# Gate logits of a four-expert layer computed with the activations as the loaded operand of TensorE

## What is computed

```python
gate_logits = jnp.einsum('bte,en->btn', x, Wg) + bg      # x: 1250 x 768, Wg: 768 x 4
top = jnp.argmax(gate_logits, axis=-1)                   # the expert of each node
h = gelu(einsum(x, W1) + b1);  y = einsum(h, W2) + b2    # per expert
out = the y of the expert that was chosen
```

## Time and profile before

| | us |
|---|---|
| median of 3 runs | 1021.78 (1020.6 to 1023.49) |
| the profiled execution | 1026.36 |
| span of its profile | 1024.5 |
| PE busy in the span | 989.0 (97%) |
| DVE busy | 598.0 (58%) |
| ACT busy | 312.9 (31%) |
| stage of the gates, first wait of PE after the heads to the first use of the gates on DVE | 451.0 to 478.07 |
| from there to the first transpose of the expert layer | 478.07 to 491.2 |

### The profile page before, as it was taken

The page is one execution under the profiler, slowest core; times in us unless marked ns, Lnnn a source line. Parts: engine busy times, 40 slices in busy tenths (PEclk is TensorE's granted clock), DMA queues, the critical chain, the costliest instruction groups (busy, mean ns, idle before and its releaser), DMA issues.

```text
span 1024.5 us, 15870 instructions
## 1 busy us (share of the span) xinstructions
PE 989.0 (97%) x5707; PEld 799.3 (78%) x5707; DVE 598.0 (58%) x1264; ACT 312.9 (31%) x888; POOL 67.5 (7%) x134
## 2 busy tenths in 40 slices
PE   7999999999999999999899999999999999999997
PEld 5777678999999999986566665667997557888884
DVE  7887799999999999995223237541111112333231
ACT  2444353665565566433111121221111110110100
POOL 2100000000000000132222211000000000000000
PEclk9999999999999999999999999999999999999999
DMA  6000010111111111016772539123001005001101
GB/s 160 2 1 1 1 55 4 48 39 38 38 48 46 52 37 37 13 59 248 219 265 86 185 124 287 46 75 118 1 1 46 1 1 171 26 30 31 31 12 51
DMA packets 40017, 69.99 MB, mean 68 GB/s; under 512 B 21074, under 2 KB 24926, under 8 KB 39448
## 3 DMA queue, kind: packets, MB, share of 16 engines
q1 hardware_dynamic: 37321, 58.85, 18.3%
q0 software_dynamic: 2080, 10.23, 3.0%
q10 hardware_dynamic: 559, 0.16, 0.1%
HBM read 50.10 MB, written 19.12 MB: 68 GB/s over the span
## 4 chain that ended last, share of the span: by engine, by line
PE 89%; DVE 4%; issue 2%; ACT 1%; DMA 1%; POOL 0%; ACTq 0%; DVEq 0%; POOLq 0%; SPq 0%
PE O L961 19%; PE pw L1127 15%; PE pc L831 8%; PE pa L1156 7%; PE O L958 6%; PE pw L1189 6%; PE ph L1052 5%; PE py L1073 5%; PE pa L1201 3%; PE pf L796 3%; PE pw L1215 2%; PE pf L831 2%; PE O L898 1%; PE pct L808 1%; PE pt L1117 1%
## 5 line engine op out<-in xcount | busy, mean ns | idle before, releaser
L961 PE MATMUL O<-X,masks 125*125 125x264 f32 x1200 | 277.5, 331 | 0.0
L958 PE MATMUL O<-X,CSR 125*125 125x132 f32 x1080 | 244.1, 226 | 0.0
L961 PEld LDWEIGHTS O<-X,masks 125*125 125x125 f32 x1200 | 220.1, 186 | 0.1
L1779 DVE SCALAR_TENSOR_TENSOR masks<-a2b,NA,CSR 125x375 fp32r<-125x375 f32 (+1 forms) x360 | 212.1, 649 | 6.3 <-PE O L961 4.8
L958 PEld LDWEIGHTS O<-X,CSR 125*125 125x125 f32 x1080 | 203.3, 188 | 0.0
L2040 DVE SCALAR_TENSOR_TENSOR UL<-pw,dinv,UH 125x768 fp32r<-125x768 f32 x20 | 20.4, 1018 | 109.6 <-ACT UH L1513 109.6
L1127 PE MATMUL pw<-W 128*125 128x384 f32 x240 | 80.8, 494 | 1.0 <-ACT W L1506 1.0
L831 PE MATMUL pc<-ohs_a,ohd 125*125 125x512 f16 x375 | 78.6, 349 | 1.6 <-DVE ohs_a L1589 1.6
L1127 PE MATMUL pw<-region,xr_or_h 128*125 128x384 f32 x240 | 77.6, 486 | 0.0
L1127 PEld LDWEIGHTS pw<-region,xr_or_h 128*125 128x125 f32 x240 | 45.0, 188 | 32.1
L1127 PEld LDWEIGHTS pw<-W 128*125 128x125 f32 x240 | 45.0, 191 | 31.8 <-issue 2.8
(11 more groups left out here) (252 smaller groups left out, 1441.8 us busy)
## 6 DMA issues: line engine op xcount, KB each, us to landing
a2b<-a_rows SPq DMA_DIRECT2D x12, 610.4 KB
W<-in_L_ffn_W SPq DMA_DIRECT2D x4, 1152.0 KB
WM<-in_L_ffn_W SPq DMA_DIRECT2D x4, 1152.0 KB
xr_or_h<-in_x SPq DMA_DIRECT2D x10, 336.0 KB
XH<-in_x SPq DMA_DIRECT2D x12, 280.0 KB
z_rows<-region SPq DMA_DIRECT2D x10, 336.0 KB
region<-y_rows SPq DMA_DIRECT2D x10, 336.0 KB
x_rows<-xr_or_h SPq DMA_DIRECT2D x10, 336.0 KB
```

Of the source, the lines that this page charges most:

```text
L958: nc.tensor.matmul(O[0:P, bank, d - d0, 2 * DP:4 * DP], CSR[:, s, d * P:(d + 1) * P], X[:, buf, s, 4:6, :].rearrange("p k d -> p (k d)"), ...
L961: ins = nc.tensor.matmul(O[0:P, bank, d - d0, 0:4 * DP], kept, X[:, buf, s, 0:4, :].rearrange("p k d -> p (k d)"), start=s == 0, stop=s == ...
L1779: nc.vector.scalar_tensor_tensor(masks[:, s, 0:(d1 - d0) * P], a2b[:, buf, d0 * P:d1 * P], NA1[:, s, bass.ds(h, 1)], CSR[:, s, d0 * P:d1 * ...
```

## The change

`gates(t)` exchanges the operands: the turned tile, 128 x 125, is loaded, and `WG` with its four columns moves. The result is nodes by experts, 125 x 4, and is written at once to its four columns of `pg`. `copy_gates`, `turn_gates`, the buffer `gT` and the semaphores `s_gc3` and `s_gt3` go. DVE (line 1694 of the new file) and SP (before it loads the experts' second biases, line 615) wait for `s_g3` of the last tile in place of `s_gt3`.

```diff
-        gT = in_side(448, N, NEXP)
...
-        s_gc3, s_gt3 = sem("gates_copied"), sem("gates_turned")
...
-                sp.wait_ge(s_gt3, NT)
+                sp.wait_ge(s_g3, NT)
...
                 def gates(t):
 
                     pe.wait_ge(s_ztc3, 2 * t + 2)
-                    if t >= 2:
-                        pe.wait_ge(s_gc3, t - 1)
                     for k in range(KF):
-                        ins = nc.tensor.matmul(pgt[0:NEXP, t % 2, 0:P], WG[:, k, :], ZT[:, t % 2, k, :],
+                        ins = nc.tensor.matmul(pg[0:P, NEXP * t:NEXP * (t + 1)], ZT[:, t % 2, k, :], WG[:, k, :],
                                                start=(k == 0), stop=(k == KF - 1))
                     ins.then_inc(s_g3, 1)
-
-                def turn_gates(t):
-
-                    pe.wait_ge(s_gc3, t + 1)
-                    nc.tensor.transpose(pg[0:P, NEXP * t:NEXP * (t + 1)], gT[:, t * P:(t + 1) * P],
-                                        ident[0:NEXP, 0:NEXP]).then_inc(s_gt3, 1)
...
                         gates(t)
-                        if t:
-                            turn_gates(t - 1)
-                    turn_gates(NT - 1)
...
-                def copy_gates(t):
-                    act.wait_ge(s_g3, t + 1)
-                    nc.scalar.copy(gT[:, t * P:(t + 1) * P], pgt[0:NEXP, t % 2, 0:P]).then_inc(s_gc3, 1)
...
                         copy_zt(t)
-                        copy_gates(t - 1)
-                    copy_gates(NT - 1)
...
-                    dve.wait_ge(s_gt3, NT)
+                    dve.wait_ge(s_g3, NT)
```

## The result

| | us | |
|---|---|---|
| median before, in the same comparison | 1022.63 | 4 runs, 1020.6 to 1023.49 |
| median after | 1034.47 | 4 runs, 1033.03 to 1036.15 |
| ratio after / before | 1.011 | 95% interval 1.0093 to 1.0128 |
| profiled execution after, its span | 1033.65, 1031.9 | before 1026.36, 1024.5 |
| mean granted clock of the runs | 0.978 to 0.980 | profiled execution before 0.994 |

The account below looks back on a forecast made before the run. PE was taken to bound the gates stage. At low clock: tiles +12.4, last gates +1.1, tail -0.65, sorting +0.7, perhaps half a microsecond back; 1021.8 + 13.3 gives about 1035 us, range 1018 to 1037.

Parts of the forecast that it names:

- (e): Gates stage: streaming falls from 81% to 32% of a tile; judged by streaming, the clock stays low; 1035 us, chance 0.50.
- Step (d): Gate instructions: bound by loads, twelve take 1.32 us at clock 1.0 (1.38 now), 2.52 at 0.5 (2.48 now).
- rival 3: Gates stage: clock stays low but loads keep 0.11 us; 2.72 us a tile, +1.7, 1023.5 us; chance 0.05.
- The term of a tile: Gates stage at low clock: transposes 1.40 plus gates 2.52, 3.92 us, 1.55 more than now; eight cycles, +12.4.
- The sorting: Fourteen line 923 matmuls start at low clock: 1.5 us extra, less 0.8 us of cover, +0.7.
- the second fall: Clock drop at about 487.5 before the change; if it doesn't happen, half a microsecond at the expert layer comes back.
- (b): Gates stage: the small transpose of line 905 leaves PE, 0.19 us a tile, eight times on the path.
- (c): End of the gates stage: the tail between last gate instruction and DVE goes; 0.65 us saved, about 0.08 left.
- Rival 4: Gates stage: path not shortened because normalised tiles, stores or biases are late; 1021 to 1022 us; chance 0.04.
- rival 1: Gates stage: loads count as work, clock returns and holds; 2.11 us a tile, -2.8, 1019.0 us; chance 0.34.

Follow-up runs that it names:

- e6: Kernel before, with 20 matmuls of 4 moving columns (loads of 125) in TensorE's wait ahead of the gates stage: 1023.24 us, ratio 1.0008 to the kernel before.
- e1: Kernel before, with nine filler matmuls of 512 columns in TensorE's wait ahead of the gates stage: 1020.79 us, ratio 0.9975 to the kernel before.
- e4: Changed kernel with gates of three of the six feature blocks only, six loads fewer a tile: 1018.32 us, single run, whole time not compared.
- e2: Changed kernel with nine fillers of 512 columns ahead of the gates stage: 1028.94 us, ratio 1.0059 to the kernel before.
- e7: Kernel before with nine fillers ahead of the stage and exchanged operands in every second tile: 1020.39 us, ratio 0.9981 to the kernel before.
- e3: As e2, plus two fillers of 512 columns after each tile's gates: 1036.54 us, ratio 1.0104 to the kernel before.
- e5: As e2, plus four fillers a tile, two after the transposes and two after the gates: 1029.37 us, ratio 1.0066 to the kernel before.

## Why the prediction was right

**The cause, (e), was right.** The clock didn't come back in the stage, as forecast for a chip that goes by streaming. The prediction could not tell from the trace of before whether loads count and gave this case a chance of a half, so choosing it was in part a bet; e6 against e1 settles it. The rows that it leaned on, the fall after 484.1 to 487.3 and the rise only after unbroken streaming, pointed the right way. Two of its readings are weaker than they sound. It counts a transpose's 0.107 us as streaming, but each transpose also loads 128 columns (PEld), so its shares of streaming are upper ones. And the earlier trace rows show that transposes held a clock that was up (609.2 to 613.4), not that they raise one: beside loads they didn't raise it in the 40.6 us here.

**Step (d) was right.** Loads end 0.21 us apart at 0.5 (2.64 us for twelve) and 0.11 at 1.0 (e6); on the path a gate took 0.19 (e4). The pair of loads in the earlier trace rows was enough to see it. With it falls rival 3, loads that keep their pace at the low clock, 0.11 us at either clock. The Trainium skill (TensorE: Matmul & The Clock Gate, LDWEIGHTS) gives a load's time without a term for the granted clock; the trace after doesn't agree with that at the low clock, 0.21 us a load.

**The term of a tile was too large.** 3.92 us were forecast and 3.67 came: eight cycles at +1.30 and not +1.55, that is 2.0 us less. The sum took over the 0.15 us between transposes and gates that the kernel before shows. That gap belongs to the old order of operands and not to the clock: from the start of the transposes to that of the gates the old order takes 0.79 us at 1.0 and 1.41 at 0.5 (e6, 450.43 to 451.84), the exchanged one 0.67 (e2, 454.44 to 455.11) and 1.28 (461.74 to 463.02). Why, no run shows; in the exchanged order the first gate load (462.82) starts while transposes still stream. The gates themselves took 2.38 us from their start to the next transposes, not 2.52. To the first use of the gates the prediction had 12.4 + 1.1 - 0.65 = +12.9, measured +10.9.

**The sorting was a little off.** +0.7 us was forecast for fillers at the low clock, less up to 0.5 if the second fall didn't come. The clock returned during the fourteen, and the table's first matmuls came 6.64 us after the first use of the gates instead of 6.02. But before, the second five of them waited for DVE until 484.82, so most of the 0.6 was absorbed there: the last nine fillers start 10.00 us after the first use for 9.87, +0.1. The prediction took the cover only up to 484.09. These nine ran at 1.0, so the expert layer started with the landing of its tile: -0.8 in all. A new fall at 501.9 then cost the first expert matmuls about 1.6 us (5.75 us for twelve, against 4.13), and a fall that the kernel before has from 624 to 627.4 (twelve matmuls in 5.80 us, 4.11 after) is missing after. The prediction had neither.

**Parts (b) and (c) happened and were drowned.** The tail shrank as forecast, from 0.73 us (477.34 to 478.07) to 0.13, where 0.08 was forecast.

**Rival 4 was put down too lightly.** The prediction read from the 7.76 us that DVE waits at the end that the normalised tiles are well ahead everywhere. That wait holds for the last tile. In the middle of the stage DVE still finishes the attention's last columns, and as soon as PE takes 1.90 us a tile it waits for ACT, and ACT for POOL (1.03 us in e2, 0.68 in e7). Had the clock held, the gain would probably have been smaller than rival 1 said; no run shows that case.

The agreement of the median, 1034.5 with 1035, is better than the steps: an excess of 2 us in the stage stood against differences of the other stretches that were not forecast. The prediction added 13.3 us to 1021.8; measured were 11.8 on top of 1022.6. The hit to 0.5 us is luck.

## What to carry to other kernels

Exchanging the operands of a small product so that the small one moves doesn't save TensorE time when the loads of the large one last as long as its streaming did; look up a pair of loads in the trace before. Ask of every change that shortens what TensorE streams whether the clock holds without it: the granted clock of the stage before, and what the engine did ahead of each fall and rise, are in the profile, and busy time doesn't tell. Where TensorE waits two microseconds ahead of a dense stage, fillers that end before the wait does can be free and keep the clock, as in e1.

## What the runs showed of the hardware

- Loads of the stationary operand don't hold TensorE's clock: with 2.00 of 2.00 us busy with twenty loads (e6) it fell as in an idle wait, with nine matmuls of 512 columns in the same place (e1) it held. In the changed kernel loads were in flight for 39.17 of 40.6 us, and it stayed at 0.50.
- A load of 125 f32 columns costs about 0.2 us at 1.2 GHz (0.21 between the ends of loads, 0.19 on the path in e4) and 0.11 at 2.4 (e6), when loads follow each other; here it follows the granted clock.
- At the high clock the stage held it for four tiles with transposes as nearly all of the streaming (e2), and lost it 1.3 us behind a wait of 1.0 us. With two fillers a tile it fell in the third tile without any wait, and three runs of four had a mean clock of 0.980, about that of the changed kernel without fillers (e3). With four fillers spread over the tile it held up to the last gates (e5).
- Unneeded work made the kernel faster: e5 has 40 filler matmuls in its tiles and 9 ahead of them that the changed kernel lacks, and its median is 5 us lower.
